# Layer norm of the query rows moved into the K/V projection, and PSUM banks of the attention stage assigned anew

## The reference

```
xn = layernorm(x)                                    # over the last axis, no weights
q = xn @ Wq                                          # 32 heads of 128
k, v = split(xn @ Wkv)                               # one k and one v of 128, shared by all heads
scores = q k^T / sqrt(128) + slope_h * (kpos - qpos), causal
s = softmax(scores) v @ Wo
g = silu(xn @ dequant(qweight, scales, zeros).T + bias)
out = x + s * g
```

## Time and profile before

| | us |
|---|---|
| median of 2 runs | 7380.45 (7376.44 to 7384.46) |
| the profiled execution | 7382.53 |
| its span, slowest core (core 7) | 7380.7 |
| spans of the 8 cores | 7333.8 to 7380.7 |
| granted clock of TensorE, mean | 0.832 to 0.836 of full |
| busy: PE / DVE / ACT / POOL | 4322.9 / 2436.1 / 1823.9 / 1014.7 |

### The profile page before, as it was taken

The page is one execution under the profiler, slowest core; times in us unless marked ns, Lnnn a source line. Parts: engine busy times, 40 slices in busy tenths (PEclk is TensorE's granted clock), DMA queues, the critical chain, the costliest instruction groups (busy, mean ns, idle before and its releaser), DMA issues.

```text
span 7380.7 us, 56060 instructions; the slowest of 8 cores (7333.8 to 7380.7 us)
## 1 busy us (share of the span) xinstructions
PE 4322.9 (59%) x18152; PEld 1770.0 (24%) x18152; DVE 2436.1 (33%) x2572; ACT 1823.9 (25%) x2712; POOL 1014.7 (14%) x787
## 2 busy tenths in 40 slices
PE   0000647775995220166566996986665668969930
PEld 0000213332442220011122443431111113434410
DVE  4444001110002442277675000006886781000012
ACT  6776000000002440034353000013553560000000
POOL 0000000000000000035353000003663670000000
PEclk9999978887996555577778998997887889989965
DMA  7777997777445889800001435440000003355578
GB/s 271 296 296 267 175 166 156 160 156 149 93 93 151 216 223 291 277 0 1 28 1 28 98 93 120 112 126 0 1 16 13 1 1 83 93 111 114 118 206 279
DMA packets 1553326, 936.98 MB, mean 127 GB/s; under 512 B 1331602, under 2 KB 1487250, under 8 KB 1520018
## 3 DMA queue, kind: packets, MB, share of 16 engines
q1 hardware_dynamic: 1243794, 648.17, 35.7%
q10 hardware_dynamic: 309248, 285.24, 12.3%
HBM read 581.01 MB, written 251.66 MB: 113 GB/s over the span
## 4 chain that ended last, share of the span: by engine, by line
PE 43%; DMA 19%; DVE 18%; issue 7%; ACT 6%; SPq 5%; POOL 0%; ACTq 0%; DVEq 0%; POOLq 0%
PE pbE L785 12%; PE pbE L835 12%; PE pqC L475 10%; DVE accA L674 9%; DMA wqrC<-wq 4%; DMA xA<-xkv 4%; DMA wobh<-wobD 3%; DMA xcF<-xq 3%; PE pbE L694 3%; ACT wfoD L544 3%; SPq L374 2%; DVE stA L300 2%; PE pbE L663 2%; PE pbfD L564 2%; ACT xnA L330 2%
## 5 line engine op out<-in xcount | busy, mean ns | idle before, releaser
L475 PE MATMUL pqC<-xntqC,wqbC 128*128 128x512 bf16 x4096 | 950.0, 397 | 313.6 <-DVE wqbC L456 257.8
L674 POOL TENSOR_TENSOR accA<-accA,ppb 128x512 f32<-128x512 f32 x719 | 975.5, 1357 | 185.3 <-ACT ppb L719 53.9
L835 PE MATMUL pbE<-attnTE,wftslE 128*128 128x512 bf16 x4096 | 888.1, 380 | 117.9 <-DMA wftslE<-wfth 117.8
L719 ACT ACTIVATE ppb<-pbE,bslE 128x512 bf16<-128x512 f32 x1264 | 782.3, 695 | 688.2 <-PE pbE L694 356.4
L674 DVE TENSOR_TENSOR accA<-accA,ppb 128x512 f32<-128x512 f32 x681 | 857.9, 1260 | 260.1 <-ACT ppb L719 114.0
L785 PE MATMUL pbE<-attnTE,woslE 128*128 128x512 bf16 x4096 | 889.8, 381 | 21.7 <-DMA woslE<-wobh 21.7
L694 PE MATMUL pbE<-qtsE,kt 128*128 128x512 bf16 x1528 | 588.4, 440 | 479.9 <-DMA tsbE<-tstk 375.5
L669 POOL CAST accA<-ppb 128x512 f32<-128x512 bf16 x64 | 39.0, 610 | 4901.2 <-ACT ppb L724 3107.0
L663 PE MATMUL pbE<-ppb,vt 128*128 128x512 bf16 x1528 | 577.0, 410 | 143.8 <-ACT ppb L719 111.9
L379 PE MATMUL pbigB<-xntB,wkv_bf 128*128 128x512 bf16 x384 | 151.6, 395 | 829.8 <-DMA xntB<-xnh 823.1
L475 PEld LDWEIGHTS pqC<-xntqC,wqbC 128*128 128x128 bf16 x4096 | 412.9, 101 | 850.7 <-issue 410.2
(11 more groups left out here) (51 smaller groups left out, 2678.9 us busy)
## 6 DMA issues: line engine op xcount, KB each, us to landing
xA<-xkv SPq DMA_DIRECT2D x48, 2048.0 KB, 10.6
xnh<-xnA ACTq DMA_DIRECT2D x64, 1024.0 KB, 10.9
wqrC<-wq SPq DMA_DIRECT2D x32, 2048.0 KB, 18.4
qwD<-qw SPq DMA_DIRECT2D x32, 2048.0 KB, 8.8
worD<-wo SPq DMA_DIRECT2D x32, 2048.0 KB, 16.3
woslE<-wobh SPq DMA_DIRECT2D x64, 1024.0 KB, 8.2
wftslE<-wfth SPq DMA_DIRECT2D x64, 1024.0 KB, 9.2
xA<-xq SPq DMA_DIRECT2D x16, 2048.0 KB, 11.3
```

The costliest lines, as they stand in the source:

```text
L475: mm_done = P.emit("tensor", lambda e, jj=j, c_=ch, p_=pb: e.matmul(pq[:, 2048 * p_ + 512 * c_:2048 * p_ + 512 * (c_ + 1)], wqb[p_][:, 128 ...
L674: ac = P.emit(eng, lambda e, pi=ppi_p, i_=i_p: e.tensor_tensor(out=accA[:, 512 * i_:512 * (i_ + 1)], in0=accA[:, 512 * i_:512 * (i_ + 1)], ...
L719: ex = P.emit("scalar", lambda e, b_=sb, pi=ppi, f_=fi, j_=j: e.activation(ppb[:, 512 * pi:512 * (pi + 1)], pb_[b_][:], AF.Exp, bias=bsl[: ...
L835: bb=bkf: e.matmul(pb_[bb + qq][:], wftsl[p_][:, 128 * g_:128 * (g_ + 1)], b_[:, c_ + 512 * qq:c_ + 512 * (qq + 1)], start=(g_ == 0), stop ...
```

## The change

1. **A and B become one stage.** The buffers of B are allocated beside those of A. The load of `wkv` and its cast are issued ahead of the first tile. The tiles are taken in the order `xkv0`, `xkv1`, `xq`. The body of the tile loop becomes a function, `emit_ln_tile`, called 48 times for the K/V tiles; then B's loop begins, and at every sixth transposing DMA, from the first on, one of the 16 tiles of `xq` is emitted ahead of it. The first four transposes wait for the stores of the K/V tiles (`aN0`, `aN1`); the stores of `xq` tiles raise semaphores of their own (`aM0`, `aM1`). The barrier between A and B is gone, that behind B stays.
2. **Banks in E.** Scores rotate over two banks for each head (0 and 1, 2 and 3), the products with V stand in banks 4 and 5, and the sum and the broadcast in 6 and 7.

```
+        if stop_phase > 1:
+            dkv = P.emit("sync", lambda e: e.dma_start(
+                out=wkv_raw[:].rearrange("p (j f) -> p j f", j=32), in_=wkv.rearrange("(j p) f -> p j f", p=128)), incs=[("bW", 16)])
+            vcast = P.emit("vector", lambda e: e.tensor_copy(out=wkv_bf[:], in_=wkv_raw[:]),
+                           waits=[("bW", dkv)], incs=[("v", 1)])
...
-        srcs = [(xq, 0, QR // 128), (xkv0, QR // 128, SLOT_E[0] // 128),
-                (xkv1, (QR + SLOT_E[0]) // 128, SLOT_E[1] // 128)]
+        srcs = [(xkv0, QR // 128, SLOT_E[0] // 128),
+                (xkv1, (QR + SLOT_E[0]) // 128, SLOT_E[1] // 128),
+                (xq, 0, QR // 128)]
...
+        for _ in range(n_kv):
+            emit_ln_tile()
+
+        if stop_phase > 1:
+            kv_ready = [P.dw("aN0"), P.dw("aN1")]
...
+                    for j in range(32):
+                        if gj[0] % 6 == 0 and ti[0] < len(tiles):
+                            emit_ln_tile()
+                        pb = gj[0] % 4
+                        lw = [("v", vcast), ("t", mmj_done.get(gj[0] - 4, 0))]
+                        if gj[0] < 4:
+                            lw = lw + kv_ready
...
-                                pb_[6 + i_][:], vt_s[s_][:, 128 * jj:128 * (jj + 1)],
+                                pb_[4 + i_][:], vt_s[s_][:, 128 * jj:128 * (jj + 1)],
...
-                            sb = 3 * i + (actidx[i] % 3)
+                            sb = 2 * i + (actidx[i] % 2)
...
-                            pb_[3 * i_][0:1, :], c_onecf[:], accA[:, 512 * i_:512 * (i_ + 1)],
+                            pb_[6 + i_][0:1, :], c_onecf[:], accA[:, 512 * i_:512 * (i_ + 1)],
...
-                        bank_free[3 * i] = ("v", rcp)
+                        bank_free[6 + i] = ("v", rcp)
...
-                        bank_free[6 + i] = ("v", mul)
+                        bank_free[4 + i] = ("v", mul)
```

More of the change, by code:

```diff
@@ L264, in build_nc @@
     rs_f = [rs_f0, rs_f0]
+    vt_tmp = {}
+    stB = ExitStack()
+    EB = stB.enter_context
+    if stop_phase > 1:
+        vt_tmp[0] = EB(nc.sbuf_tensor("vtt0", [128, SLOT_E[0]], BF16))
+        vt_tmp[1] = EB(nc.sbuf_tensor("vtt1", [128, SLOT_E[1]], BF16))
     with ExitStack() as stA:
@@ L271, in build_nc @@
         stt = [EA(nc.sbuf_tensor(f"stA{i}", [128, 8], F32)) for i in range(2)]
+        if stop_phase > 1:
+            xnt = [EA(nc.sbuf_tensor(f"xntB{i}", [128, 2048], BF16)) for i in range(4)]
+            wkv_raw = EA(nc.sbuf_tensor("wkv_raw", [128, 32 * 256], F32))
+            wkv_bf = EA(nc.sbuf_tensor("wkv_bf", [128, 32 * 256], BF16))
+            pbig = EA(nc.psum_tensor("pbigB", [128, 4096], F32))
         for dst, src in ((c_ident, ident), (c_bbase, bbase),
@@ L287, in build_nc, with emit_ln_tile @@
                 tiles.append((src, base_t + tloc, tloc))
+        n_kv = (SLOT_E[0] + SLOT_E[1]) // 128
         last_use = [None, None]
-        xnb_guard = [0, 0]
-        sq_guard = [0]
-        for i, (src, trow, tloc) in enumerate(tiles):
+        xnb_guard = [("aN0", 0), ("aN1", 0)]
+        ti = [0]
+        def emit_ln_tile():
+            i = ti[0]
+            ti[0] += 1
+            src, trow, tloc = tiles[i]
             pb = i % 2
+            wstream = (f"aN{pb}" if i < n_kv else f"aM{pb}")
             waits = []
@@ L331, in build_nc @@
                 xnb[p_][:], xb[p_][:], AF.Identity, scale=st[:, 6:7], bias=st[:, 7:8]),
-                waits=[("v", v5), ("s", s3), (f"aN{pb}", xnb_guard[pb])], incs=[("s", 1)])
-            dxn = P.emit("scalar", lambda e, p_=pb, tr=trow: e.dma_start(
+                waits=[("v", v5), ("s", s3), xnb_guard[pb]], incs=[("s", 1)])
+            dxn = P.emit("scalar", lambda e, p_=pb, tr=trow, ws=wstream: e.dma_start(
                 out=xnh[128 * tr:128 * (tr + 1), :], in_=xnb[p_][:]),
-                waits=[("s", s4)], incs=[(f"aN{pb}", 16)])
+                waits=[("s", s4)], incs=[(wstream, 16)])
@@ L338, in build_nc @@
+        while ti[0] < len(tiles):
+            emit_ln_tile()
         P.barrier()
     if stop_phase <= 1:
[L340 to L343, removed]
         _emit_taps(nc, P, taps, scratch)
@@ L347, in build_nc @@
         return nc
[L349 to L414, removed]
@@ L736, in build_nc @@
                         dmms[i] = P.emit("tensor", lambda e, i_=i: e.matmul(
-                            pb_[3 * i_][0:1, :], c_onecf[:], accA[:, 512 * i_:512 * (i_ + 1)],
+                            pb_[6 + i_][0:1, :], c_onecf[:], accA[:, 512 * i_:512 * (i_ + 1)],
                             start=True, stop=True),
-                            waits=[last_ac[i], bank_free[3 * i]], incs=[("t", 1)])
+                            waits=[last_ac[i], bank_free[6 + i]], incs=[("t", 1)])
                         acc_guard[i] = ("t", dmms[i])
@@ L742, in build_nc @@
                         rcs[i] = P.emit("vector", lambda e, i_=i: e.reciprocal(
-                            out=rd_f[i_][:], in_=pb_[3 * i_][0:1, :]),
+                            out=rd_f[i_][:], in_=pb_[6 + i_][0:1, :]),
                             waits=[("t", dmms[i]), ("v", rcb_guard[i])], incs=[("v", 1)])
```

59 lines of the change are left out of this document (54 added, 5 removed).

## The result

The changed kernel is faster by 1.0%: its ratio to the kernel before is 0.9898, 95% interval 0.9857 to 0.994. On the 7380.45 us shown before, that is 7305 us, where 7259 was forecast with a range of 7190 to 7335. The raw median of its 19 runs is 7485.18 us (7302.23 to 7770.46), above that range; the raw median of 18 runs of the kernel before, taken with them, is 7451.12 us. In about half of the runs of the kernel before, and in more of the changed kernel's, cores of one die or of both ran for a time at a lower granted clock, which the ratio leaves out; the profile of the changed kernel is from such a run (cores 2 to 5 in the Q projection, cores 0, 1, 6 and 7 in the products behind attention), so only stages in which PE's clock sets nothing are read from it.

The account below looks back on a forecast made before the run. The prediction took transposing DMAs to bound the K/V projection and DVE's chain attention, with no layer-norm engine full. From 7382.5 us it subtracted 64 and 58 for 7260.5, about 7259 against the run median; range 7190 to 7335.

Parts of the forecast that it names:

- What bounds each stage: Layer norm: no engine full; K/V projection: transposing DMAs, share 1.02; attention: DVE's adds and two reciprocals per pair.
- The tiles gone from A, 171 us gained, and the weights' load at the head, 17 lost: Layer norm: 16 tiles at 10.71 us leave, 171.4 us; moving weight load and cast saves 21.2, costs 17.
- B grows by 112 us: K/V projection: 16 tiles add 129 us of DMA work, less 17 for transposes cheaper when mixed.
- part 1: Moving 16 of 64 layer-norm tiles under the K/V projection's transposes: 64 us gained, bounds 47 and 81.
- PE's clock in the pauses, ACT's copies behind the statistics, at most 15 us: K/V projection: slower PE after pauses and ACT's PSUM copies delayed at block ends; cost taken 0, at most 15 us.
- Two score banks cost nothing: Attention: losing the third score bank is free, since PE's earlier V matmul already waits for the same exp.
- Attention gains 58 us: Next pair's scores no longer wait for the broadcast's copy: 20 near changes at 1.3 us, 40 far at 0.8.
- Rival 1: Attention gives nothing: GpSimd holds DVE's adds whichever starts first, or copy and multiply stretch; 7317 us, chance 0.20.
- second form: Attention: GpSimd's earlier first cast slows DVE's copy and multiply, each from 0.69 to 1.46 us, 1.5 us a pair.
- Rival 2: Attention: GpSimd gets a whole add ahead, DVE's last add runs alone; 46 us more gained, 7213 us, chance 0.10.
- Rival 3: K/V projection: DMA share is time held, not work, so the tiles add nothing; 7147 us, chance 0.06.
- Rival 4: K/V projection: loads and transposes do not mix in one queue, 16 x 16.5 = 264 us; 7404 us, chance 0.07.

Follow-up runs that it names:

- p1_only: Only the merged layer norm and K/V projection, with the old PSUM banks, against the kernel before: ratio 0.9948 (0.9898 to 0.9998), attention 2060 us.
- p2_only: Only the new PSUM banks in attention, with the old stages, against the kernel before: fastest run 7411.1 us beside 7451.33, attention 1993 us.

## Why the prediction was right or wrong, point by point

- **What bounds each stage:** right. The DMA share of B on core 7 is 0.96 to 1.05 in every kernel, whatever is put into it, more buffers change nothing, and attention followed DVE's chain.
- **The tiles gone from A, 171 us gained, and the weights' load at the head, 17 lost:** right. The first transpose was forecast for 554.7 and came at 551.1.
- **B grows by 112 us:** wrong in size, and this is the step that failed. It grew by 158 (444.6 - 286.4), and by 160 on one chip (`p1_only` 461.2, `p2_only` 301.5). The term was made of 89 us for 15 loads, 40 for 16 stores, and 17 off because the transposes were to be cheaper when mixed. On one chip the loads were worth 102 and the stores 50, and the transposes did not get cheaper: 112 + 13 + 10 + 17 = 152, and the last 6 us are within the scatter of B. The prices came from the layer norm, where no transposes ran, and the discount from the last stage, where another pattern runs. Beside transposes at a full share, a store costs 3.1 us instead of 2.49 and a load 6.8 instead of 5.94; why both get dearer there stays open. The bounds of part 1, 47 to 81 us gained, were too narrow; 18 came in the profiles, and 22 on the chip of `p1_only`.
- **PE's clock in the pauses, ACT's copies behind the statistics, at most 15 us:** right at nothing that shows; seven buffers (460 us against 456) and the kernel without tiles (307 against 301 with the old stages) show it.
- **Two score banks cost nothing:** right, shown by putting the sum back.
- **Attention gains 58 us:** right in mechanism, a little low. 67 came, 1.44 and 0.95 us a change instead of 1.3 and 0.8.
- **Rival 1** (attention gives nothing) fell. Its second form is answered too. GpSimd's first cast or its first add now overlaps 98 of the 256 copies and multiplies on core 7, where before it overlapped none, and each of these takes 690 to 693 ns. Over attention of slot 0 the means are the 692 ns that they were:

```profile
L777 DVE TENSOR_TENSOR attnTE<-pbE,rs_f 128x512 bf16<-128x512 f32 x64 | 44.3, 692 | 7.4 <-DVE rs_f L772 0.9
L772 DVE COPY rs_f<-pbE 128x512 f32<-128x512 f32 x64 | 44.3, 692 | 19.8 <-PE pbE L767 16.1 <-PE pbE L708 0.5
```

 The rule of the Trainium skill that was weighed there ("SBUF — State Buffer", Who interferes with whom) agrees with these rows.
- **Rival 2** (GpSimd ahead, DVE's last adds alone) fell: the median add is 1455 ns as before, and of the last adds of the 64 pairs on core 7 none runs under 900 ns; their median is 1454 ns, where it was 1453.
- **Rival 3** (the tiles hide wholly) fell: B grew by 158. With it falls what the rule of the Trainium skill ("Advanced Engine Details and Errata", X-Bar Transpose (TRN2)), that transposing DMAs are as fast as regular ones, would have meant here: without tiles the transposes cost 5.91 us a MB.
- **Rival 4** (loads and transposes do not mix) was nearer the truth than its 0.07. Each load does hold up the issue of the next transpose until about its own landing. Only the price was not the 16.5 us assumed: the next transpose lands 2 us behind the end of its issue and not 5.9, so a tile costs 9.6 to 9.9 us, under the 10.7 it cost in A.
- **The total:** 64 + 58 = 122 us were forecast; 18 + 67 = 85 came by the stages, and 75 by the ratio. The 7305 us that the ratio gives lie in the range of 7190 to 7335, but by its width and not by its reasons: they are outside the 7225 to 7290 of the forecast itself, since part 1 gave 18 us and not 64.

## What to carry to other kernels

When work is moved under a stage whose DMA engines are full, only the difference of two prices is gained: here 10.7 us for a tile in a stage where no engine was full against 9.6 of engine time, 10% of what was moved. Take the price from a stretch where the same kinds of DMA run beside each other, and take no discount from another pattern. Before hiding a load, ask whether it is needed: leaving out the doubled rows took 173 us off A and B, and hiding them 22, on the same chip.

## What the runs showed of the hardware

- A transposing DMA issued after a plain 2 MB load in the same queue took 8.0 to 11.2 us to issue in all 15 places instead of mostly 2 to 4, about until the load had landed, with the DMA engines held all the while (share 1.10). With the load in the other queue it was 15.45 us in the case shown, and the transposes' price was 7.60 us a MB instead of 5.9 for transposes by themselves.
- Beside stores of 8 KB rows the transposes cost 6.43 us a MB.
- DVE's reciprocal of 512 elements takes 3.31 us on one partition and 3.35 on two.
- A DVE add of two SBUF tiles takes 0.69 us where no GpSimd add or cast overlaps it and 1.46 in the median where one does; DVE's copy and multiply from PSUM kept their 0.69 beside a GpSimd cast or add.
